# Four-layer graph network at edge ends: the projection rewritten with DVE square roots and index gathers four at a time, and the map-row gathers moved beside the first aggregation

## What is computed

```python
def _L0_gnn_ref(x, edge_index, Ws, att_src, att_dst, bias):
    def _gat_conv(x, src, dst, W, a_src, a_dst, b, n_nodes):
        h = x @ W
        s = h @ a_src
        d = h @ a_dst
        e = s[src] + d[dst]
        e = jnp.where(e > 0, e, NEG_SLOPE * e)
        ...
        out = jax.ops.segment_sum(alpha[:, None] * h[src], dst, num_segments=n_nodes)
        return out + b
    ...
    for m in range(Ws.shape[0]):
        x = x + jax.nn.sigmoid(_gat_conv(x, src, dst, Ws[m], att_src[m], att_dst[m], bias[m], n))
    return x
...
h = jnp.maximum(_layernorm(x, axis=-1), 0.0)
x = x + _L0_gnn_ref(h, edge_index, L0_gnn_Ws, ...)
```

## Time and profile before

| | us |
|---|---|
| median of 3 runs | 4023.5 (4010.86 to 4040.4) |
| profiled execution, its own time | 4039.1 |
| its span | 4037.4 |
| `setup`, `keys` and `local_chain` | 0 to about 1312 |
| project round 0, "first" | 1312 to 1514.6 |
| `rows_found` and `attend` | 1514.6 to 1538.9 |
| aggregate round 0 | 1538.9 to about 1679 |
| project round 1, "plain" | 1681 to 1889.5 |
| project round 2, "plain" with x | 2028 to 2236.5 |
| project layer 2, "normed" | 2762.2 to 2970 |
| `edge_messages`, `edge_outputs` | 3160 to 4037 |

### The profile page before, as it was taken

One profiled execution on the slowest core, in us unless ns is written; L12 is line 12 of the kernel. 1 busy time (PEld: TensorE's weight loads), 2 busy tenths in 40 slices (PEclk: granted clock), 3 DMA queues, 4 the chain that ended last, 5 costly groups with the idle time before them and its releaser, 6 DMA issues. The chain is left out here.

```text
span 4037.4 us, 57894 instructions
## 1 busy us (share of the span) xinstructions
PE 2352.2 (58%) x13633; PEld 1865.0 (46%) x13633; DVE 2246.1 (56%) x7631; ACT 1625.7 (40%) x3515; POOL 2168.0 (54%) x1921
## 2 busy tenths in 40 slices
PE   1136899899897664455646557775635433444333
PEld 1023676667677553354546445444624322333222
DVE  4145998899997665323422448885676323333223
ACT  0006999999995663222422323323421222222100
POOL 3628765566554770152055245555820488788755
PEclk9998999999999786587678668887866666666666
DMA  2140132233321543642455363333413433332243
GB/s 62 28 174 24 43 97 91 85 108 90 95 68 45 135 129 86 160 115 78 127 145 138 86 178 99 93 89 89 113 29 90 119 72 72 73 73 64 50 142 113
DMA packets 569016, 380.34 MB, mean 94 GB/s; under 512 B 51389, under 2 KB 511942, under 8 KB 568386
## 3 DMA queue, kind: packets, MB, share of 16 engines
q1 hardware_dynamic: 510050, 329.99, 27.7%
q0 software_dynamic: 56000, 46.29, 6.1%
q10 hardware_dynamic: 2720, 1.23, 0.2%
HBM read 249.08 MB, written 153.32 MB: 100 GB/s over the span
## 5 line engine op out<-in xcount | busy, mean ns | idle before, releaser
L1147 POOL DMA_INDIRECT p_ends_state<-t_d,p_ends_ix x300 | 315.6, 1052 | 543.9 <-issue 243.7
L806 POOL TENSOR_TENSOR a_rs<-a_ve,w_neg_half 128x16 f32<-128x16 f32 x113 | 330.4, 2924 | 244.8 <-DVE a_ve L742 214.9
L1367 PE MATMUL p_pm<-w_aug,p_ht 128*128 128x130 f32 (+1 forms) x1600 | 331.8, 329 | 173.0 <-ACT p_ht L1321 117.2
L832 ACT ACTIVATE a_nr<-a_xb,a_nm,a_rs 128x128 f32<-128x128 f32 x882 | 371.6, 490 | 26.1 <-POOL a_nm L808 26.1
L1367 PEld LDWEIGHTS p_pm<-w_aug,p_ht 128*128 128x128 f32 x1600 | 275.7, 234 | 194.9 <-issue 137.3
L1983 POOL DMA_INDIRECT e_a<-t_d,e_ix x200 | 211.7, 1059 | 269.7 <-DMA e_a<-t_s 206.9
L894 PE MATMUL a_ps<-w_ident,a_nr 128*128 128x128 f32 x1568 | 248.1, 282 | 127.8 <-ACT a_ht L840 46.9
L902 PE MATMUL a_ps<-a_ht,w_aug 128*128 128x512 f32 x588 | 315.6, 622 | 2.4 <-DVE a_ht L709 2.4
L894 PEld LDWEIGHTS a_ps<-w_ident,a_nr 128*128 128x128 f32 x1568 | 181.6, 144 | 276.7 <-issue 245.1
L709 DVE TENSOR_TENSOR a_ht<-a_ps,a_ht 128x512 f32<-128x512 f32 x294 | 203.1, 694 | 137.4 <-ACT a_ps L847 119.2
L1708 PE MATMUL c_pq<-layer_src,c_sel 128*128 (+1 forms) x800 | 194.3, 420 | 126.7 <-ACT c_sel L1679 83.5
(11 more groups left out here) (359 smaller groups left out, 6657.2 us busy)
## 6 DMA issues: line engine op xcount, KB each, us to landing
t_s<-p_ends_state SPq DMA_DIRECT2D x100, 256.0 KB
c_a<-t_d SPq DMA_DIRECT2D x100, 256.0 KB
t_d<-c_a SPq DMA_DIRECT2D x100, 256.0 KB
a_xa<-in_x SPq DMA_DIRECT2D x98, 256.0 KB
out<-a_xb SPq DMA_DIRECT2D x98, 256.0 KB, 2.0
p_ends_state<-t_s SPq DMA_DIRECT2D x75, 256.0 KB
p_ends_state<-t_d SPq DMA_DIRECT2D x75, 256.0 KB
t_acc<-q_zt SPq DMA_DIRECT2D x3, 2171.5 KB
```

What stands on the lines that cost most here:

```text
L806: nc.gpsimd.tensor_tensor(RS[:, z, :], VE[:, z, :], w["neg_half"][:, None, 0:J].to_broadcast([P, LNS, J]), ALU.pow).then_inc(s_rstd.sem, 1)
L832: last = nc.scalar.activation(NR[k][:, T.at(NORM[k], 2), cols(j)], normed_rows(T, k)[:, cols(j)], ACT.Identity, bias=NM[:, T.at(1, SHORT), ...
L1147: eng.indirect_dma_start(out=self.A[:, g, SRC, j, :], out_offset=None, in_=self.t[self.dst_table], in_offset=bass.IndirectOffsetOnAxis(ap= ...
L1367: last = nc.tensor.matmul(PM[side][:, j, 0:CW], HT[:, g, side, j * C:(j + 1) * C], rhs, start=side == SRC, stop=True)
```

## The change

`project` is written anew, without `stream`, `Ends` and `Norms`, and fully unrolled over the 25 blocks:

- The ring of loaded rows has 7 slots in place of 5, with three slots for the small intermediates. SP issues seven pairs of loads, then the stores in order; the loads for block b+6 stand behind the store of block b.
- Gathers take their index straight from `map_ix`; the index copies are gone. Each of the four lanes j has a semaphore of its own, and before a gather POOL waits until the previous gather of the same lane has landed. So at most four are in flight.
- Norms (new class `Moments`) no longer use POOL: DVE computes 1/sqrt by three Newton steps from a bit-level first guess. There are twelve steps (13 small operations on 128x8) per block, standing between the eight statistics and eight aggregates of the next block. ACT applies the norm to all eight tiles; in "first" the relu is part of it.
- The bias matmuls are gone. DVE holds both products and adds the bias to both.
- Lags: with norms the products are held 3 blocks and the residual added 4 blocks after the statistics; without norms 0 and 1.
- The gathers of map rows move out of "first" into `aggregate` of round 0 (new L1665), again in four lanes with a wait each, and straight into their table; `rows_found` moves behind that `aggregate` and makes three more copies, since the table is of integers now.

Core of the diff:

```diff
+    def newton(self, eng, b, step):
...
+        if step == 0:
+            eng.wait_ge(self.s_moments, b + 1)
+            v.tensor_scalar(ve, self.moments[:, g, :, 1], LN_EPS, None, ALU.add).then_inc(self.s_newton, 1)
+            return
+        eng.wait_ge(self.s_newton, b * (self.STEPS - 1) + step)
+        if step == 1:
+            v.tensor_scalar(half, ve, -0.5, None, ALU.mult)
+            v.tensor_scalar(y.bitcast(I32), ve.bitcast(I32), -0.5, 1597463007.0, ALU.mult, ALU.add).then_inc(self.s_newton, 1)
+        elif step == self.STEPS - 1:
+            v.scalar_tensor_tensor(self.shift[:, g, :], self.moments[:, g, :, 0], -1.0, y, ALU.mult, ALU.mult).then_inc(self.s_shift, 1)
+        elif step % 3 == 2:
+            v.tensor_tensor(square, y, y, ALU.mult).then_inc(self.s_newton, 1)
+        elif step % 3 == 0:
+            v.tensor_tensor(square, square, half, ALU.mult).then_inc(self.s_newton, 1)
+        else:
+            v.scalar_tensor_tensor(y, square, 1.5, y, ALU.add, ALU.mult).then_inc(self.s_newton, 1)
...
+            for b in range(RING):
+                load(b)
...
+            for b in range(BLOCKS):
+                store(b)
+                if b and b - 1 + RING < BLOCKS:
+                    load(b - 1 + RING)
...
+                for b in range(BLOCKS):
+                    g = b % RING
+                    eng.wait_ge(s_load[g], uses(b) * 32)
+                    for j in range(J):
+                        if b:
+                            eng.wait_ge(s_over[j], 16 * b)
+                        eng.indirect_dma_start(out=A[:, g, SRC, j, :], out_offset=None, in_=t[f"d{r}"],
+                                               in_offset=bass.IndirectOffsetOnAxis(ap=k["map_ix"][:, b * J + j:b * J + j + 1], axis=0),
+                                               bounds_check=EP - 1, oob_is_err=False).then_inc(s_over[j], 16)
...
+            holds, residuals = (3, 4) if norm else (0, 1)
+            for n in range(BLOCKS + residuals):
+                if norm and n <= BLOCKS:
+                    if n < BLOCKS:
+                        there(eng, n)
+                    mo.turn(eng, lambda m: A[:, n % RING, m // J, m % J, :], n, BLOCKS - 1)
+                if 0 <= n - residuals:
+                    residual(n - residuals)
+                if 0 <= n - holds < BLOCKS:
+                    hold(n - holds)
...
+        if first:
+            s_found = [sem(f"found{j}") for j in range(J)]
+
+            @block.gpsimd
+            def _(eng):
+                for n in range(T):
+                    lane, turn = n % J, n // J
+                    if turn:
+                        eng.wait_ge(s_found[lane], 16 * turn)
+                    eng.indirect_dma_start(out=f["found"][:, n, :], ...).then_inc(s_found[lane], 16)
```

More of the change, by code:

```diff
@@ L1167, in project @@
+def project(nc, w, k, t, r, heads, rhs, bias_row, kind, plus_x, keep):
     CW = C + 2 * heads
-    sigmoid = kind != "normed"
-    norm = kind != "plain"
+    first, normed = kind == "first", kind == "normed"
+    sigmoid, norm, overlay = not normed, kind != "plain", not first
+    RING, SHORT = 7, 3
     with phase(nc) as ctx:
@@ L1191, in project @@
-        OUTS = 32 if kind == "first" else 16
-        if kind == "first":
-            ROWS = ctx.enter_context(nc.sbuf_tensor(pre + "map_rows", [P, GE, J, WORDS], I32))
-            s_map = [sem(f"map{g}") for g in range(GE)]
-            s_found = sem("found")
+        s_bias, s_tp, s_ht, s_sig, s_next, s_plus = (sem(n) for n in "bias tp ht sig next plus".split())
+        s_normed, s_mm, s_keep = ([sem(f"{n}{side}") for side in ("src", "dst")] for n in ("normed_", "mm_", "keep_"))
+        s_load, s_out = ([sem(f"{n}{g}") for g in range(RING)] for n in ("load", "out"))
@@ L1374, in attend @@
+                    last.then_inc(s_mm[side], 1)
+            products = 1 if norm else 0
+            for n in range(BLOCKS + products):
+                if n < BLOCKS:
+                    turn(n)
+                if 0 <= n - products:
+                    product(n - products)
 def attend(nc, w, k, r, heads, keep, wm, ws, whole):
```

294 lines of the change are left out of this document (150 added, 144 removed).

## The result

The changed kernel takes 4054.0 us (median of 15 runs, 4040.7 to 4072.8) against 4026.8 us (15 runs): a ratio of 1.0069, 95% interval 1.0049 to 1.0090. So it is slower, by little but clear of the noise; it was forecast at 3885.

A forecast was written before the change was run, and what follows sets the result against it. POOL was taken to bound the first projection, and late PE counts during POOL's long gather runs the plain ones. −42 − 53 − 53 + 3 + 6 = −139 from 4023.5 gave 3885 us, range 3835 to 3955.

The forecast's parts named there:

- What stays is POOL's own work, if four in flight keep the counts moving: Plain projections: POOL's 100 gathers at 1.30 us and the ends set the time, 155.5 us against 208.5.
- its pace of 1.30 us per gather is hardly broken, just as in the bad runs: Argument for late PE counts persisting with four gathers in flight: POOL's stream has hardly a pause.
- the normed projection shows no such wait: Argument against late counts persisting: with eight gathers in a row, then fours, ACT had no such wait there.
- First aggregation, +6 forecast: Adding 100 map gathers beside the first aggregation takes it to 1684 on the timeline: +6 us, from 0 to +28.
- The first rival: Four in flight doesn't cure late counts: aggregation +90 us, plain projections stay at 208.5, total 4075; chance 0.10.
- Plain projections, −53 each forecast: Each plain projection falls from 208.5 to 155.5 us; ends −60 and −33.
- the term for slower gathers: Plain projections: one gather per block beside the residual takes 1.33 us in place of 1.00, 8 us in all.
- Normed projection, +3 forecast: Normed projection goes from 208 to 211 us, set by the ring's loop; ends −31 and +12.
- The loop of the ring: Normed projection: block b+6's load stands behind block b's store; 16.6 us per two turns, 8.3 each, for 18 blocks.
- the start and the end: Normed projection: 12 us at the start, 7 × 5.7 for the ring's first blocks, 10 at the end.
- First projection, −42 forecast: POOL leaves the stage and DVE sets it at 5.7 us per block: 160 us against 202.6; ends −55 and 0.
- The second rival: Large DVE operations each stretch a gather by 0.33 us: +16.5 per plain projection, aggregation +22, total 3940; chance 0.17.

The follow-up runs named there:

- e9_nolanes_again: Changed kernel without the four lanes' waits: ratio 1.0099 to the kernel before; the same version earlier, on the chip without late counts, 0.9855.
- e1_add4: Changed kernel plus an unused POOL addition of 128x8 (0.2 us) behind every four gathers: ratio 1.0042 to the kernel before.
- e18_all8_half: Changed kernel, map gathers divided, ten normed ring slots, unused 128x4 POOL power behind every eight gathers and `keys` scatters: 3852.1 us against 3997.8 before, 0.9627.
- e13_keys_too: Changed kernel, map gathers divided, ten normed ring slots, unused 128x8 POOL power behind every four gathers and `keys` scatters: 3906.2 us against 4009.7 before, 0.9750.
- e2_pow4: Changed kernel plus an unused POOL power of 128x8 (1.67 us) behind every four gathers: ratio 1.0008 to the kernel before.
- e3_drain4: Changed kernel, but POOL waits before each four gathers until all of the four before have landed: ratio 1.0299 to the kernel before.

## Why the prediction was wrong

**The step that failed** is "What stays is POOL's own work, if four in flight keep the counts moving". The number in flight isn't what decides; `e9_nolanes_again` has no limit and the same holds. What decides is whether POOL's stream of gathers has a break of about a microsecond or more every four to eight: 0.2 us (`e1_add4`) is not enough, 1.0 is. A break also slows the mean pace, from 1.36 us per gather (`e1_add4`, past its first twelve) to 1.48 (`keys` of `e18_all8_half`); no run keeps the one and changes the other, so whether the break or the pace lets the counts through stays open. A lane's wait ended before POOL came to it nearly always (the stream went on at 1.30 us), so it made no break. I had written this against myself ("its pace of 1.30 us per gather is hardly broken, just as in the bad runs") and set against it that the normed projection shows no such wait. That was the wrong use of the earlier trace rows: the row between the fours, a power of 1.67 us, was the cure and not the number four. The change took just this row away from all projections, and added the one stream of 100 gathers to a stage that had none.

**First aggregation, +6 forecast, +77 measured.** The first rival's mechanism and nearly its price (+90). Seven blocks passed while POOL gathered, as the rival had it. The others then followed at 3.9 us in place of the 5.6 it took, which makes it less than +90.

**Plain projections, −53 each forecast, −21.5 and −21 measured.** The rest of the sum was right, by one profile: on the chip without holds they took 147.5 and 151.5 us with no limit, against 147.5 without the term for slower gathers and 155.5 with it. The rival had them unchanged; the gain that remained comes, as I read it, with the ring of seven, whose longer runs make fewer stops of POOL (in round 1 four of over 2 us, where there were ten); that wasn't tested by itself.

**Normed projection, +3 forecast, +30 measured.** The loop of the ring is as worked out. POOL's waits for the loads stand two blocks apart, 16.9 us, against 16.6 taken:

```profile
2823.92 1.00 POOL L1307 DMA_INDIRECT p_a<-t_d,k_map_ix  x1 [7.26 <-DMA p_a<-t_d]
...
2840.77 0.99 POOL L1307 DMA_INDIRECT p_a<-t_d,k_map_ix  x1 [6.76 <-DMA p_a<-t_d]
```

A ring of ten takes 39 us out (`e13_keys_too` against `e2_pow4`, which has seven slots and the same pauses). What I missed is the start and the end. The ring's first seven blocks are 28 gathers in one stream, and along it DVE waits for its own counts, as shown above, and then POOL stands still for 22.68 us:

```profile
2806.34 1.00 POOL L1307 DMA_INDIRECT p_a<-t_d,k_map_ix  x1 [22.68 <-DMA p_a<-t_d]
```

The first seven turns of DVE (first to eighth group of L1203) took 57 us where I had 40; on the chip without holds they took 39 (`e9_nolanes`), and there DVE has no wait for itself. So these 17 us are the same fault as in the aggregation. Behind the start of the last turn stood 20 us, not 10, on both chips: that term was mis-sized. The 18 turns between took 144 us (149 taken), the first load 14 (12 taken), which makes the 24 us missed. Without lanes on both, the stage took 225.1 us without holds and 251.4 with them (`e9_nolanes_again`).

**First projection, −42 forecast, −46 measured.** The groups on DVE, in the form of the earlier trace rows:

```profile
L1203 DVE BATCH_NORM_STATS2 p_mo_st<-p_a 128x6 f32<-128x128 f32 x200 | 54.1, 285 | 4.3 <-DMA p_a<-t_xd 4.3
L1213 DVE BATCH_NORM_AGGREGATE p_mo_mv<-p_mo_st 128x2 f32<-128x6 f32 x200 | 21.6, 162 | 0.0
...
L1190 DVE TENSOR_TENSOR p_mo_sq<-p_mo_rs 128x8 f32<-128x8 f32 x75 | 10.8, 145 | 0.1
```

A Newton operation takes 0.145 us and they wait for nothing between the statistics; after the first four the turns came at 4.9 and about 6.3 us alternately, 5.6 on average against 5.7.

**The second rival** (a shared door between gathers and DVE) is cheap, if it is a door: beside 37 products of DVE in one stream at the start of the first aggregation a gather takes 1.50 us in place of 1.00, twelve times, some 6 us. The mean of the 300 in the projections is 1.013 us (before 1.052), by the page of the changed kernel:

```profile
L1307 POOL DMA_INDIRECT p_a<-t_d,k_map_ix x300 | 303.9, 1013 | 491.9 <-DMA p_a<-t_d 394.1
```

The Trainium skill ("SBUF — State Buffer", section "SBUF: two separate sides") says that a transfer issued by GpSimd takes about 3100 ns in place of 620 beside a DVE copy. These are products and not copies, and beside them the trace shows half as much again and not five times, but for one gather of `e3_drain4`, which took 13.30 us, the only one of its kind. Timelines of DVE and of POOL in the changed kernel, and of POOL in `e3_drain4`:

```profile
1483.41 15.14 DVE L1693 TENSOR_TENSOR layer_src<-layer_src,layer_edge_weight 128x512 f32<-128x512 f32 x25 [1.01 <-PEq L43]
```

```profile
1503.93 1.50 POOL L1665 DMA_INDIRECT f_found<-t_maps,f_map_at  x1 [0.30 <-issue]
1505.74 0.99 POOL L1665 DMA_INDIRECT f_found<-t_maps,f_map_at  x1 [0.30 <-issue]
```

```profile
1491.85 13.30 POOL L1667 DMA_INDIRECT f_found<-t_maps,f_map_at  x1 [2.35 <-DMA f_found<-t_maps,f_map_at]
```

**Range and chances.** The range ended 99 us short. It held the door rival, which cost little, and left the first rival outside at a chance of 0.10. That rival's sum, 4075, is 21 us from the measured 4054; partly by luck, since it had no gain in the plain projections and no loss but 3 us in the normed one. Its row of `keys` was the only one that showed POOL in one stream beside a loop like the aggregation's, and deserved most of the weight for that stage. The band that came true, within 1% of the kernel before, had a chance of 0.04.

## What to carry to other kernels

A stream of transfers issued by POOL is not only POOL's time: look at what the other engines hand over while it runs, to each other and to themselves. If an engine starts late on work long done and its releaser is a transfer long past, move the stream to where nothing is handed over, or put a microsecond of other work into it every four to eight transfers. And before taking a "wasteful" instruction off an engine, ask what its time keeps apart. Compare such a change on more than one chip, with the kernel before beside it each time.

## What the runs showed of the hardware

- While POOL issues gathers or scatters in one stream (1.30 us each), results of PE reach DVE late, growing along the stream to 18 us (PE's matmuls end at 1575.1, DVE begins at 1592.9). DVE's own counts reach DVE late as well (20 waits of up to 3.7 us in the normed projection), while the gathers' own counts come within 5.2 us.
- A POOL operation of 1.0 us or more every four gathers ends it as far as the waits show. One every eight, of 1.7 or 1.0 us, ends it in `keys` and leaves small waits elsewhere (up to 1.4 us of DVE for itself, and with 1.0 us once 4.3 us for a product). In the aggregation 0.2 us every four does nothing, nor does a limit of four in flight. The mechanism below this stays open: no run shows which path the counts and the descriptors share, or whether they share one.
- It isn't so on every chip. On one chip the same kernels ran without any such delay (the kernel before 3835 us in place of 3998 to 4027 on the others), gathers at the same 1.30 us. In `keys` alone 72 us lie between the two. Whether that lies in the chip or in its state at that time isn't shown: all its runs stood in one group.
